# A recurrence scanned two chunks at a time, with the initial state written into PSUM by ScalarE

## The reference, cut to what matters

```
s0 = state[:, i0 + 2:i0 + 2 + S].reshape(B, H, S, S)

def step(s, inp):
    k_l, v_l, w_l, r_l = inp
    a = k_l[..., :, None] * v_l[..., None, :]
    out = jnp.einsum('bhs,bhst->bht', r_l, faaaa * a + s)
    s_new = a + w_l[..., None] * s
    return (s_new, out)
```

## Time and profile before

| | us |
|---|---|
| median of three executions | 4551.24 |
| lowest, highest | 4549.75, 4553.67 |
| the profiled execution, its own time | 4558.4 |
| its span, first to last instruction | 4556.6 |
| one turn of phase C's loop | 115.9 |
| POOL's power in a turn | 10.56 |

### The profile page before, as it was taken

How to read it: one execution, slowest core, us unless ns; L and a number is a source line. 1 busy time by engine, 2 the same in 40 slices (tenths; PEclk the granted TensorE clock), 3 DMA queues, 4 the chain that set the end, 5 groups by cost and what they waited for, 6 DMA issues and landing times. The chain is left out here.

```text
span 4556.6 us, 71467 instructions
## 1 busy us (share of the span) xinstructions
PE 3786.7 (83%) x21636; PEld 2917.4 (64%) x21636; DVE 3071.6 (67%) x6716; ACT 2022.0 (44%) x5336; POOL 1897.6 (42%) x1162
## 2 busy tenths in 40 slices
PE   5888888588888886999999778888888888888865
PEld 4777777366666664899999555555555555555533
DVE  5777777477777774656565267777677777677772
ACT  4666666366666664555454312222222222222211
POOL 2444444133333332000000136666666666666653
PEclk8999999799999997999999879999999999999987
DMA  3334434244334433010101210000000000000000
GB/s 110 91 93 100 97 92 97 85 117 106 97 97 105 106 102 118 28 41 28 41 28 37 93 28 13 22 22 22 22 22 22 21 18 21 16 22 22 22 17 14
DMA packets 146610, 256.58 MB, mean 56 GB/s; under 512 B 27184, under 2 KB 32048, under 8 KB 145424
## 3 DMA queue, kind: packets, MB, share of 16 engines
q1 hardware_dynamic: 146448, 254.49, 20.6%
HBM read 107.62 MB, written 33.55 MB: 31 GB/s over the span
## 5 line engine op out<-in xcount | busy, mean ns | idle before, releaser
L1199 POOL TENSOR_TENSOR c_S<-c_S,c_rT 128x1024 f32<-128x1024 f32 x256 | 557.3, 2177 | 495.2 <-DVE c_S L1474 488.0
L1474 DVE TENSOR_TENSOR_SCAN c_S<-c_wT,c_s,c_vb 128x256 f32<-128x256 f32 x1024 | 709.1, 735 | 45.0 <-issue 2.7
L1469 DVE TENSOR_TENSOR c_vb<-c_kT,c_vb 128x512 f32<-128x512 f32 x512 | 353.2, 690 | 455.8 <-PE c_vb L1637 422.9
L348 POOL TENSOR_TENSOR x_prob<-x_prob,x_rsums 128x512 f32<-128x512 f32 x256 | 274.4, 1072 | 543.1 <-DVE x_rsums L511 543.1
L348 POOL TENSOR_TENSOR s_prob<-s_prob,s_rsums 128x512 f32<-128x512 f32 x256 | 274.7, 1073 | 488.7 <-DVE s_rsums L511 488.7
L404 ACT ACTIVATE x_prob<-x_t,x_tmin 128x256 f32<-128x256 f32 x512 | 256.5, 502 | 280.4 <-DVE x_tmin L504 280.4
L404 ACT ACTIVATE s_prob<-s_t,s_tmin 128x256 f32<-128x256 f32 x512 | 256.4, 501 | 248.6 <-DVE s_tmin L504 248.6
L1637 PE MATMUL c_vb<-c_vhl,c_spread 128*128 128x512 f32 x512 | 305.2, 606 | 72.3 <-DVE c_S L1474 59.7
L867 PE MATMUL b_ps<-b_ln_high,b_w_high 128*128 128x256 f32 x1024 | 291.1, 284 | 15.0 <-DVE b_ln_low L809 15.0
L869 PE MATMUL b_ps<-b_ln_high,b_w_low 128*128 128x256 f32 x1024 | 291.0, 284 | 0.0
L868 PE MATMUL b_ps<-b_ln_low,b_w_high 128*128 128x256 f32 x1024 | 291.0, 284 | 0.0
(11 more groups left out here) (258 smaller groups left out, 10897.1 us busy)
## 6 DMA issues: line engine op xcount, KB each, us to landing
s_stack<-s_parts_qk SPq DMA_DIRECT2D x384, 128.0 KB, 2.4
x_stack<-x_parts_qk SPq DMA_DIRECT2D x384, 128.0 KB, 2.4
s_x_in<-in_x SPq DMA_DIRECT2D x16, 512.0 KB, 3.6
s_xb<-in_x SPq DMA_DIRECT2D x16, 512.0 KB, 4.1
x<-s_x_out SPq DMA_DIRECT2D x16, 512.0 KB, 4.8
x_enc<-in_ctx SPq DMA_DIRECT2D x16, 512.0 KB, 4.4
x_x_in<-x SPq DMA_DIRECT2D x16, 512.0 KB, 3.7
x_xb<-x SPq DMA_DIRECT2D x16, 512.0 KB, 4.2
```

The costliest lines, as they stand in the source:

```text
L348: nc.gpsimd.tensor_tensor(prob[:, h % 4, :, :], prob[:, h % 4, :, :], rsums[:, h, :].unsqueeze(2).to_broadcast([P, TC, T]), ALU.mult).then ...
L1199: nc.gpsimd.tensor_tensor(S[:, n % 4, :, 0:T], S[:, n % 4, :, 0:T], rT[:, par, :, :], ALU.mult).then_inc(z_ready, 1)
L1469: nc.vector.tensor_tensor(pair(vb, i), pair(kT[:, par, :, :], i), pair(vb, i), ALU.mult)
L1474: op = nc.vector.tensor_tensor_scan(S[:, n % 4, c, 1:T + 1], wT[:, par, c, :], vb[:, c, :], s0[:, par, c, n:n + 1], ALU.mult, ALU.add)
```

## The change

Everything is shifted by one column. The operand of the scan now has the initial state in column 0 of each chunk and k times v of token t-1 in column t, and the decay has a zero in column 0. A scan over both chunks of a half laid end to end (128x512) then starts afresh at each chunk: 0 times the running value plus s0.

- `S` has 256 columns to a chunk, and is one dense block of 1024 for POOL.
- `recur` waits for `a0_ready` in place of `vb_filled` (and `s0_loaded`), multiplies 2x255 elements, and issues one scan in place of two, with a constant as initial value.
- `start_state` is called twice a step, once a half. It waits for `vb_filled` of that half, and writes a column of two values into `vb`. Its first call stands at the head of the step, ahead of the reads of the second list of step n-1, and its second call where the old one stood.
- `wT`, `vhl` and `vlow` are written from column 1 on; POOL clears their column 0 once, at the start of phase C.
- POOL no longer waits for `a0_ready`.

```diff
                     for n in range(RS):
                         if "wkv" in parts:
-                            pool.wait_ge(a0_ready, step(k, n))
                             pool.wait_ge(scanned, half(k, n, 1))
-                            nc.gpsimd.tensor_tensor(S[:, n % 4, :, 0:T], S[:, n % 4, :, 0:T], rT[:, par, :, :],
+                            nc.gpsimd.tensor_tensor(S[:, n % 4, :, :], S[:, n % 4, :, :], rT[:, par, :, :],
                                                     ALU.mult).then_inc(z_ready, 1)
...
-                            nc.scalar.activation(wT[:, other, :, :], wT[:, other, :, :], ACT.Exp, scale=-1.0).then_inc(w_ready, 1)
+                            nc.scalar.activation(wT[:, other, :, 1:T], wT[:, other, :, 1:T], ACT.Exp, scale=-1.0).then_inc(w_ready, 1)
...
-                        nc.scalar.copy(pair(vhl[:, other, 0, :, :], i), channels(name)).then_inc(vh_ready, 1)
+                        nc.scalar.copy(pair(vhl[:, other, 0, :, :], i)[:, :, 1:T], channels(name)[:, :, 0:T - 1]).then_inc(vh_ready, 1)
...
-                def start_state(k, n, par):
-
-                    if n == 0:
+                def start_state(k, n, i, par):
+
+                    if n == 0 and i == 0:
                         act.wait_ge(s0_loaded, 16 * k + 16)
-                    if not first(k) or n >= 4:
-                        act.wait_ge(summed, k * (RS // 2) + ((n - 4) // 2 + 1))
-                    nc.scalar.copy(S[:, n % 4, :, 0], s0[:, par, :, n]).then_inc(a0_ready, 1)
+                    act.wait_ge(vb_filled, half(k, n, i))
+                    nc.scalar.copy(pair(vb, i)[:, :, 0], s0[:, par, 2 * i:2 * i + 2, n]).then_inc(a0_ready, 1)
 
                 def body(k, parts, par):
                     for n in range(RS):
+                        if "wkv" in parts:
+                            start_state(k, n, 0, par)
                         if n > 0:
                             take(k, FILLS[n - 1][1], parts, par)
...
                         if "wkv" in parts:
-                            start_state(k, n, par)
+                            start_state(k, n, 1, par)
                         take(k, FILLS[n][0], parts, par)
...
                 def recur(k, n, i, par):
 
                     if n == 0 and i == 0:
-                        dve.wait_ge(s0_loaded, 16 * k + 16)
                         dve.wait_ge(w_ready, k + 1)
-                    dve.wait_ge(vb_filled, half(k, n, i))
-                    nc.vector.tensor_tensor(pair(vb, i), pair(kT[:, par, :, :], i), pair(vb, i), ALU.mult)
+                    x = pair(vb, i)[:, :, 1:T]
+                    dve.wait_ge(a0_ready, half(k, n, i))
+                    nc.vector.tensor_tensor(x, pair(kT[:, par, :, :], i)[:, :, 0:T - 1], x, ALU.mult)
                     nc.vector.drain()
                     if i == 0 and (not first(k) or n >= 4):
                         dve.wait_ge(summed, k * (RS // 2) + ((n - 4) // 2 + 1))
-                    for c in (2 * i, 2 * i + 1):
-                        op = nc.vector.tensor_tensor_scan(S[:, n % 4, c, 1:T + 1], wT[:, par, c, :], vb[:, c, :],
-                                                          s0[:, par, c, n:n + 1], ALU.mult, ALU.add)
-                    op.then_inc(scanned, 1)
+                    nc.vector.tensor_tensor_scan(flat(pair(S[:, n % 4, :, :], i)), flat(pair(wT[:, par, :, :], i)),
+                                                 flat(pair(vb, i)), 0.0, ALU.mult, ALU.add).then_inc(scanned, 1)
```

More of the change, by code:

```diff
@@ L967, in phase_c @@
         s0 = sb("s0", P, 2, KC, RS)
-        S = sb("S", P, 4, KC, T + 1)
+        S = sb("S", P, 4, KC, T)
         b0, b1, b2 = sb("b0", P, KC, T), sb("b1", P, KC, T), sb("b2", P, KC, T)
@@ L1149, in _ @@
                 nc.gpsimd.memset(gather[:, :], 0.0)
+                nc.gpsimd.memset(wT[:, :, :, 0:1], 0.0)
+                nc.gpsimd.memset(vlow[:, :, 0:1], 0.0)
+                nc.gpsimd.memset(vhl[:, :, :, :, :].rearrange("p a s c n -> p (a s c) n").bitcast(F32)[:, :, 0:1], 0.0)
                 nc.gpsimd.drain()
@@ L1298, in move @@
                         for c in range(2):
-                            op = nc.scalar.activation(wT[:, other, 2 * i + c, :], channels(name)[:, c, :], ACT.Exp,
+                            op = nc.scalar.activation(wT[:, other, 2 * i + c, 1:T], channels(name)[:, c, 0:T - 1], ACT.Exp,
                                                       bias=col(w["cols"], "time_decay", 2 * i + c))
@@ L1430, in read @@
                         dve.wait_ge(emptied["act"], units.emptied(k + 2, "bonus1"))
-                        nc.vector.tensor_tensor(pair(vlow, i).bitcast(F32R), u, pair(vhl[:, other, 0, :, :], i), ALU.subtract)
+                        nc.vector.tensor_tensor(pair(vlow, i)[:, :, 1:T].bitcast(F32R), u[:, :, 0:T - 1],
+                                                pair(vhl[:, other, 0, :, :], i)[:, :, 1:T], ALU.subtract)
                         nc.vector.tensor_tensor(pair(bonusT[:, other, :, :], i), u, pair(bonusT[:, other, :, :], i),
@@ L1648, in sum_states @@
                             op = nc.tensor.matmul(pair(acc, i)[32 * tile:32 * tile + 32, :, :],
-                                                  gather[:, 24 - 8 * o:56 - 8 * o], pair(S[:, n % 4, :, 0:T], i),
+                                                  gather[:, 24 - 8 * o:56 - 8 * o], pair(S[:, n % 4, :, :], i),
                                                   start=(o == 0), stop=(o == 3))
```

## The result

The changed kernel takes 4570.52 us (median of 6 runs, 4568.66 to 4576.39), the kernel before 4552.39 (6 runs beside them, 4539.78 to 4556.82). The ratio is 1.0044, 95% interval 1.0031 to 1.0058: slower, by 18 us, where 3.4 us faster had been forecast. In the profiled pair it is 10.3 us (spans 4556.6 and 4566.9).

A forecast was written before the change was run, and what follows sets the result against it. No engine was full; the bound moved between DVE, POOL and PE. Thirteen turns at -0.16 us (-2.1), item 14's turn -0.64, first and last turns -0.6: about -3.4, so 4547.8 us, range 4535 to 4572.

The forecast's parts named there:

- Scan: DVE's recurrence: one scan of 512 columns replaces two of 256 (1.38 us), a gain of 0.16 us a half.
- column: ACT's copy of two values into PSUM, between `vb` and DVE's multiplication: 0.15 to 0.20 us.
- POOL's product: POOL's multiplication of the dense S before its power: 2.35 us, +0.17 a turn.
- order: Step 13: ACT writes the column before normalising ln1, so `xaT` starts 2.26 us behind the `vb`: mean +0.48 a turn.
- three places of the hop: Added wait through ACT's column, 0.21 us each, counted where DVE waits for `vb`: once each in stretches A, D, E.
- D: Steps 7 and 8, DVE-bound: one wait of 0.21 less two halves' gain of 0.32 gives -0.11 us a turn.
- at step 4: ACT's reading of `zT` begins 1.4 us late, hidden by a projection except in the last turn, which loses 1.4.
- scan's split: DVE scan of 256 columns, 736 ns: fixed 184, column operand 27 (up to 45), and 2.05 ns a column.
- A: Steps 0 to 2, taken as DVE-bound: 0.21 us of wait less five halves at 0.16, so -0.59 a turn.
- E's first part: Step 11 to step 13's first `vb`: 0.21 us of wait less two halves at 0.16, so -0.11 a turn.
- Clock: PE behind `xaT` at step 13: taken as full, with 0 added from `xaT` to the first projection.
- Rival 1: Slower: a second pause at step 13 makes PE's low clock last twice as long, +17.4 us, 4565; chance 0.15.

The follow-up runs named there:

- the quiet pair: Kernel before and changed kernel, each with filler matmuls on PE, five calls at step 13 and 18 at step 4: 4523.91 and 4530.76 us.
- e7_two_copies: Changed kernel with the column written twice by ACT, a drain between: 4579.02 us (one run).
- e5_pool_adds: Changed kernel with three short operations on variances and means moved from DVE to POOL: 4538.23 us, 0.9980 of the kernel before.
- e6_all: Changed kernel with step 13's normalisation ahead of the column, r padded to 257 columns, and DVE's three short operations on POOL: 4517.30 us, 0.9933 of before.

## Why the prediction was wrong

- **Scan, column, POOL's product, order: right.** 1.22 us (1.22 to 1.25 given), ACT's column 0.16 (0.15 to 0.20), 2.36 (2.35), `xaT` 2.20 behind the `vb` (2.26). The three places of the hop held, D gained the 0.13 that a hop and two halves give (0.11 forecast), and at step 4 only the last turn lost. In the scan's split one term was mis-sized: the column operand 62 ns and not 27 to 45, and the fixed part less than 184; the two errors cancelled.
- **A: wrong, -0.24 in place of -0.59.** The step that failed is "DVE works without a pause ... DVE-bound". It did, but one of its operations could not end before POOL's product ended, and the prediction looked at neither. DVE and POOL were level there before the change. Two gains of 0.16 and POOL's 0.18 put the addition 0.54 ahead of the product's end, and it lasted 0.40 longer.
- **E's first part: wrong, +0.06 in place of -0.11.** The same hold at step 11, where POOL's product starts on a scan and grew by as much as the scan shrank; only the hop and one half were left. The trace of before had the rows of it: 0.37 to 0.77 us for an addition of two columns that takes 0.17 elsewhere.
- **Order: right in kind, over-sized in the mean.** +0.32 measured for +0.48: the low turns of before had a mean `vb` to `xaT` of 2.02 and not the 1.89 of rows 6.
- **Clock: the step that decided.** The sum ends at `xaT` ("what follows is full PE, so it is lost") and puts nothing for the clock behind it; there it lost 1.00 a turn, 13 of the 13.1 us. Rival 1 had this mechanism and place, with 17 us at a chance of 0.15. Its argument against ("the same 2.8 us of idling left the clock full") took three turns of 13 for a margin; with the late start no turn was spared. Putting the old order back took 22 us off, and filling the pause 19. Rival 1 was part right: the low stretch lasted twice as long in four turns and not in all, and three falls were new.
- By the quiet pair the change costs 7 to 8 us without the clock: wrong sign even so. Of the 0.81 a turn between the forecast of -0.16 and the +0.65 there, A has 0.36, E's first part 0.17, and the order 0.29, since with a clock that never falls each turn pays 0.77 (the prediction had 0.83 for such turns, and three of 13 of them). The other 10 or so of the 18 us are the clock. Why four turns fell for twice as long and nine once is open: the long falls began 1.3 to 1.5 us behind the `vb`, the others at 0.9 to 1.2, at 1.6 or at 2.1 to 2.4.

## What to carry to other kernels

Before counting a gain on an engine's row, compare its short SBUF-only operations with the same shape elsewhere in the trace. Here an addition took 0.39 us where its shape takes 0.17; it was waiting for POOL, and a faster DVE only waited longer. Such a wait shows as a long duration and not as idle time. Where PE's clock falls behind a pause in most turns, an order of work that adds a second pause close behind is priced by the fall and not by the added wait. Test it with filler work in the pause, which also gives traces quiet enough to read 0.05 us, and size the filler from a measured call.

## What the runs showed of the hardware beyond this

- A scan costs 674 ns at 256 columns and 1221 at 512: 2.14 ns a column and 127 fixed; an initial value from a column adds 62.
- POOL's product of 1024 elements takes 2.36 us with all operands dense and 2.18 with one of them in rows of 257.
- The clock falls behind shorter pauses too, in some turns. Behind D's pause of 1.58 us it fell in two turns of the kernel before (27.02 for 25.56), and behind 1.41 in three of `e7_two_copies`. Behind a pause of 1.7 us in front of `y` it fell in all six turns of `e5_pool_adds` that have it (`y` to S2 8.80 to 9.36 for 8.60) and in five of six of `e6_all`.
